# Merging the weight folds of a convolution chain into its pointwise stage, with the first bands of the large convolution loaded inside it

## The chip, the cores and the metric

One NeuronCore of a Trainium2 chip runs the whole program. The metric is device time in microseconds of one execution. Abbreviations: PE is TensorE, DVE is VectorE, ACT is ScalarE, POOL is GpSimd, SP is SyncE. SPq and ACTq in the rows are the sequencers of SyncE and ScalarE, which issue DMAs.

## The reference

Two layers over 16 images of 192 channels, 56 by 56, float32. Only the first layer's first step and its constants are touched here:

```python
y = jnp.einsum('bchw,oc->bohw', x, pw_w)
x_pw = bn(y, pw_g, pw_b, pw_m, pw_v) + x
out = bn(dwconv(x_pw, dwk_w), dwk_g, dwk_b, dwk_m, dwk_v)          # 13x13 depthwise
out = out + bn(x_pw * dw1_w.reshape(1, -1, 1, 1), dw1_g, dw1_b, dw1_m, dw1_v)
return jax.nn.gelu(out, approximate=False)
```

`bn` is y * g / sqrt(v + eps) + (b - m * g / sqrt(v + eps)). The second layer is an attention-like block: two norms, two small depthwise mixes (5x5, 3x3, 1x1 kernels summed), a recurrence and a feed-forward part. All of it stands behind the first layer.

## The kernel before

`build` calls the stages in order, each a block of its own with one instruction list for each engine; a block ends only when all engines are through, and the next begins then: `prepare`, `pointwise`, `depthwise` (the 13x13 convolution), norm scales, `omni`, `attention`, norm scales, `omni`, `feed_forward`.

`prepare` folds constants. SyncE issues 16 loads (L200), VectorE clears the flat tap tables (L214, L215), waits for all 16 loads on one semaphore, and folds: scales and shifts of the three norms (L224 to L229), the pointwise weights with scale and identity (L232, L234), the output weights (L236, L237), the 13x13 taps (L243), the 5x5 taps (L252 to L260), their edge sums (L267 to L273). Every step waits for the one before. ScalarE takes the roots and an exponential between (L281 to L284), waits for the last fold, and stores five tables and the bias row to DRAM (L286 to L291), as the later stages read them from there.

`pointwise` works image by image with two input buffers `xin` and two output buffers `xp` (2.41 MB an image each way). SyncE loads image b+2 when PE is through with image b. PE computes 14 pairs of columns an image, four products each (L334), into one of 7 PSUM banks (L301) in turn. VectorE adds the shift and moves the bank to `xp` (L347), which frees it; at the start of image b it first waits for the store of image b-2, which used the same `xp`. ScalarE waits for an image's last evacuation and issues its store to `xpw_d` (L359).

`depthwise` goes over 24 groups of 8 channels with two buffers. For each group SyncE loads the input (L418), the bias (L422) and the bands, which are overlapping windows of the flat tap table `f13_d` (two DMAs of 56 partitions, L133). It first waits until GpSimd has cleared the margins of the band buffers (L467). ScalarE rounds the bands (L516) and the input (L521) of the first channel after it has waited for all loads of the group, GpSimd makes the rests (L473, L477), and PE multiplies (L87 to L89).

The DMAs that SyncE issues go by one queue (q1 in the page), those of ScalarE by another (q10).

Of the kernel before, what the change touches and what calls it, by code (L numbers as in the profile page):

```python
# [141 lines left out]
def prepare(nc, ins, keep, wpw, shift_pw, f13_d, f5a_d, f5f_d, sa_d, sf_d, bias_d):  # L142

    with ExitStack() as ctx:
        m = Mem(nc, ctx)
        bcv = m.sb("bcv", [128, NV, C])
# [11 lines left out]
        run = m.sb("f5_running", [CT, 2, KT, 1 + l5])  # L158
        box = m.sb("f5_box", [CT, l5])
        edge = m.sb("f5_edge", [CT, 2, KT, n5])  # L160
        sd = m.sb("sd", [128, 3, C])
        sc = m.sb("sc", [128, 3, C])
        sh = m.sb("sh", [128, 3, C])
# [5 lines left out]
        loads = m.sem("prep_loaded")  # L169
        var_ready = m.sem("prep_variances")  # L170
        root = m.sem("prep_roots")
        step = m.sem("prep_steps")
        expo = m.sem("prep_exponentials")
        stored = m.sem("prep_stored")
        block = ctx.enter_context(nc.Block())
        folds = [0]

        @block.sync
        def _(sp):
            n = 0  # L180
            vecs = ins["vecs"]
            for dst, src in [
                (bcv[:, :, :], dram(vecs, 0, [[0, 128], [1, NV * C]])),
                (colv[:, :, :], ins["vec_cols"]),
                (alph[:, :], dram(ins["alphas"], 0, [[0, CT], [1, 8]])),
                (keep.ident[:, :], ins["ident"]),
                (wpw[:, :, :], ins["pw_wt"].rearrange("(k p) n -> p k n", p=CT)),
                (keep.w_low[:, :, :], ins["att_low"]),
                (keep.w_end[:, :, :], ins["att_ends"]),
                (keep.wo[:, :, 0:C], ins["att_out"]),  # L190
                (rates[:, :, :], ins["att_rates"]),
                (dwk[:, :, :], ins["dwk_w"].rearrange("(k p) n -> p k n", p=CT)),
                (w5[:, 0], ins["att_w5"].rearrange("(k p) n -> p k n", p=CT)),
                (w5[:, 1], ins["ffn_w5"].rearrange("(k p) n -> p k n", p=CT)),
                (w3[:, 0], ins["att_w3"].rearrange("(k p) n -> p k n", p=CT)),
                (w3[:, 1], ins["ffn_w3"].rearrange("(k p) n -> p k n", p=CT)),
                (w1[:, 0], ins["att_w1"]),
                (w1[:, 1], ins["ffn_w1"]),
            ]:
                sp.dma_start(dst, src).then_inc(loads, 16)  # L200
                n += 16
            folds[0] = n

        @block.vector
        def _(dve):
            done = [0]

            def link(ins_):

                done[0] += 1  # L210
                ins_.then_inc(step, 1)
                dve.wait_ge(step, done[0])

            link(dve.memset(f13[:, :, :], 0.0))  # L214
            link(dve.memset(f5[:, :, :, :], 0.0))  # L215
            dve.wait_ge(loads, folds[0])
            dve.tensor_scalar_add(sd[:, :, :], bcv[:, 0:3, :], BN_EPS).then_inc(var_ready, 1)
            dve.tensor_scalar_add(cd[:, :, :], colv[:, :, 0:3], BN_EPS).then_inc(var_ready, 1)

            link(dve.tensor_scalar_mul(keep.decay[:, :, :], rates[:, :, 0:2], 1.0 / HW))  # L220
            dve.scalar_tensor_tensor(uw[:, :, :], rates[:, :, 2:4], 1.0 / HW,
                                     keep.decay[:, :, :], ALU.mult, ALU.add).then_inc(var_ready, 1)
            dve.wait_ge(root, 2)
            link(dve.reciprocal(sd[:, :, :], sd[:, :, :]))  # L224
            link(dve.tensor_mul(sc[:, :, :], bcv[:, 3:6, :], sd[:, :, :]))
            link(dve.tensor_mul(sh[:, :, :], bcv[:, 9:12, :], sc[:, :, :]))
            link(dve.tensor_sub(sh[:, :, :], bcv[:, 6:9, :], sh[:, :, :]))
            link(dve.tensor_copy(shift_pw[:, :], sh[:, 0, :]))
            link(dve.tensor_add(sd[:, 0, :], sh[:, 1, :], sh[:, 2, :]))  # L229

            for k in range(KT):
                link(dve.tensor_mul(wpw[:, k, :], wpw[:, k, :], sc[0:CT, 0, :]))  # L232
                own = wpw[:, k, k * CT:(k + 1) * CT]
                link(dve.tensor_add(own, own, keep.ident[0:CT, 0:CT]))  # L234
            for n in range(3):
                link(dve.tensor_mul(keep.wo[:, n, 0:C], keep.wo[:, n, 0:C], bcv[:, V["gamma1"], :]))  # L236
            link(dve.tensor_reduce(keep.wo[:, :, C], keep.wo[:, :, 0:C], AX_X, ALU.add))  # L237

            link(dve.reciprocal(cd[:, :, :], cd[:, :, :]))
            link(dve.tensor_mul(cs[:, :, :], colv[:, :, 3:6], cd[:, :, :]))  # L240
            link(dve.tensor_mul(c1[:, :], colv[:, :, V["dw1_w"]], cs[:, :, 2]))
            for k in range(KT):
                link(dve.tensor_scalar(taps_view(f13[:, k, :], K13, c13),  # L243
                                       dwk[:, k, :].rearrange("p (a b) -> p a b", a=K13),
                                       cs[:, k, 1:2], None, ALU.mult))
                mid = f13[:, k, c13:c13 + 1]
                link(dve.tensor_add(mid, mid, c1[:, k:k + 1]))

            for s in range(2):
                a = [alph[:, 4 * s + n:4 * s + n + 1] for n in range(4)]  # L250
                for k in range(KT):
                    link(dve.tensor_scalar(taps_view(f5[:, s, k, :], K5, c5),  # L252
                                           w5[:, s, k, :].rearrange("p (a b) -> p a b", a=K5),
                                           a[3], None, ALU.mult))
                    inner = taps_view(f5[:, s, k, :], K3, c5)
                    link(dve.scalar_tensor_tensor(inner, w3[:, s, k, :].rearrange("p (a b) -> p a b", a=K3),
                                                  a[2], inner, ALU.mult, ALU.add))
                    mid = f5[:, s, k, c5:c5 + 1]
                    link(dve.scalar_tensor_tensor(mid, w1[:, s, k:k + 1], a[1], mid, ALU.mult, ALU.add))
                    link(dve.tensor_add(mid, mid, a[0]))  # L260

            link(dve.memset(run[:, :, :, 0:1], 0.0))
            for s in range(2):
                gain, bias = V[f"ln{s + 1}_g"], V[f"ln{s + 1}_b"]
                for k in range(KT):
                    taps = f5[:, s, k, :]
                    link(dve.tensor_tensor_scan(run[:, s, k, 1:1 + l5], taps, free(run[:, s, k, 0:1], [[0, l5]]), 0.0,  # L267
# [11 lines left out]
        def _(act):  # L279
# [12 lines left out]
            act.wait_ge(stored, 96)  # L292


def pointwise(nc, B, x, wpw, shift_pw, xpw_d):

    with ExitStack() as ctx:
        m = Mem(nc, ctx)
# [1459 lines left out]
```

## Time and profile before

| | us |
|---|---|
| median of 3 runs | 5809.89 |
| lowest, highest | 5807.37, 5811.38 |
| the profiled execution's own time | 5813.4 |
| span of the profiled execution, first to last instruction | 5811.6 |
| PE busy | 4955.2 (85%) |
| DVE busy | 3771.1 (65%) |
| POOL busy | 3556.7 (61%) |
| ACT busy | 3493.3 (60%) |

The profile is one execution. Busy time counts instructions in work, not waits. The share of an engine is an average over stages with different limits, so each stage is read by itself: the timeline shows instructions in order with the idle time before each and what ended it; the table of stretches gives the busy time of each engine, the granted clock of TensorE, the mean busy share of the 16 DMA engines and the bytes that they moved. A DMA's line shows when it was issued; the time from issue to landing stands apart.

### The profile page before, as it was taken

The page shows a single profiled execution, that of the slowest core. Times are in us where ns is not written, and L with a number is a line of the kernel's source. Part 1 is how long each engine was busy: PE and PEld are TensorE (multiplying, and loading weights), DVE is VectorE, ACT ScalarE, POOL GpSimd, SP SyncE. Part 2 cuts the span into 40 slices and gives each one's busy share as a digit, 9 for nine tenths or more (in the row PEclk, how much of TensorE's full clock was granted, in tenths as well). Part 3 has the DMA queues.
Part 4 walks back from the last instruction along what each step waited for, and adds up shares of the span by engine and source line. Part 5 has one row for each costly group of instructions (what it writes and reads, how often), then busy time and mean ns, then how long its engine had stood idle before and what let it go on. Part 6 is the DMA issues. An engine that isn't in the chain of part 4 may idle for free. (4 is left out here: it accounts for less than half of the span.)

```text
span 5811.6 us, 78329 instructions
## 1 busy us (share of the span) xinstructions
PE 4955.2 (85%) x23504; PEld 3915.4 (67%) x23504; DVE 3771.1 (65%) x5591; ACT 3493.3 (60%) x6892; POOL 3556.7 (61%) x2992
## 2 busy tenths in 40 slices
PE   5979999979966776766867764997999999999999
PEld 5969999967733343443433434776888888888888
DVE  4423333367769999999999994774555555555555
ACT  0017777746656776766767764665555556665555
POOL 0027777757768888888888882775444444444444
PEclk9989999989988888988989887998999999999999
DMA  6987777689830321312223115997223223222320
GB/s 167 264 209 198 184 197 183 163 208 260 249 84 20 82 56 45 84 45 73 67 55 80 45 34 142 263 263 183 56 56 89 56 58 84 60 56 72 73 55 25
DMA packets 388598, 674.50 MB, mean 116 GB/s; under 512 B 21117, under 2 KB 346702, under 8 KB 368910
## 3 DMA queue, kind: packets, MB, share of 16 engines
q1 hardware_dynamic: 334768, 514.71, 38.1%
q10 hardware_dynamic: 53522, 156.21, 7.2%
q8 instruction: 130, 2.13, 0.1%
q14 instruction: 178, 1.46, 0.1%
HBM read 437.00 MB, written 233.87 MB: 115 GB/s over the span
## 5 line engine op out<-in xcount | busy, mean ns | idle before, releaser
L1545 POOL TENSOR_TENSOR hidden_part<-hidden_whole,hidden_part 128x448 fp32r<-128x448 f32 x672 | 752.8, 1156 | 1030.7 <-ACT hidden_part L1510 1029.9
L676 POOL TENSOR_TENSOR omni_in_part<-omni_norm,omni_in_part 113x448 fp32r<-113x448 f32 x384 | 609.1, 1598 | 202.7 <-ACT omni_in_part L735 199.7
L1414 PE MATMUL f_out_ps<-hidden_part,ffn_wv_parts 128*128 128x448 f32 (+1 forms) x3360 | 721.5, 370 | 0.7 <-POOL hidden_part L1545 0.7
L1414 PEld LDWEIGHTS f_out_ps<-hidden_part,ffn_wv_parts 128*128 128x128 f32 (+1 forms) x3360 | 578.6, 177 | 103.9 <-POOL hidden_part L1545 33.5
L1588 DVE TENSOR_SCALAR hidden_whole<-f_hid_ps 128x448 f32<-128x448 f32 x672 | 417.6, 622 | 254.2 <-POOL hidden_part L1545 149.3
L1038 PE MATMUL proj_ps<-mixT_low,kvr_weights_low 128*128 128x448 f32 x672 | 360.9, 622 | 214.7 <-ACT k_all L1102 184.1
L87 PE MATMUL omni_ps<-omni_in_part,omni_band_part 113*112 113x448 f32 x1152 | 438.8, 381 | 113.0 <-POOL omni_in_part L676 78.9
L1040 PE MATMUL proj_ps<-mixT_ends,kvr_weights_ends 128*128 128x448 f32 x1008 | 519.7, 599 | 0.0
L87 PE MATMUL dw_ps<-dw_in_part,dw_band_part 112*112 112x432 f32 (+3 forms) x1344 | 474.4, 353 | 42.6 <-POOL dw_in_part L477 42.6
L1203 POOL TENSOR_TENSOR input_times_v<-input_factor,v_all 128x448 f32<-128x448 f32 x336 | 420.3, 1251 | 93.2 <-ACT input_factor L1107 74.3
L88 PE MATMUL dw_ps<-dw_in_part,dw_band_part 112*112 112x432 f32 (+3 forms) x1344 | 474.7, 353 | 0.0
L89 PE MATMUL dw_ps<-dw_in_part,dw_band_part 112*112 112x432 f32 (+3 forms) x1344 | 472.0, 351 | 0.0
L473 POOL TENSOR_TENSOR dw_band_part<-dw_band,dw_band_part 112x784 fp32r<-112x784 f32 x192 | 335.0, 1745 | 191.9 <-ACT dw_band_part L516 191.8
L88 PE MATMUL omni_ps<-omni_in_part,omni_band_part 113*112 113x448 f32 x1152 | 436.8, 379 | 0.0
L89 PE MATMUL omni_ps<-omni_in_part,omni_band_part 113*112 113x448 f32 x1152 | 436.4, 379 | 0.0
L494 DVE TENSOR_TENSOR dw_sums<-dw_sums,dw_out 112x448 f32<-112x448 f32 x192 | 121.5, 633 | 456.6 <-ACT dw_out L545 456.6
L1414 PE MATMUL f_hid_ps<-ffn_mixT_part,ffn_wk_high 128*128 128x448 f32 x1344 | 397.3, 377 | 7.6 <-DVE hidden_whole L1588 6.2
L1510 ACT ACTIVATE hidden_part<-hidden_whole 128x448 fp32r<-128x448 f32 x672 | 389.2, 579 | 21.3
L516 ACT ACTIVATE dw_band_part<-dw_band 112x784 fp32r<-112x784 f32 x192 | 163.6, 852 | 390.8 <-DMA dw_band<-flat 383.8
L1040 PEld LDWEIGHTS proj_ps<-mixT_ends,kvr_weights_ends 128*128 128x128 f32 x1008 | 194.9, 207 | 278.7 <-issue 278.7
L1508 ACT ACTIVATE hidden_whole<-hidden_whole 128x448 f32<-128x448 f32 x672 | 379.8, 565 | 3.6 <-DVE hidden_whole L1588 2.0
L1038 PEld LDWEIGHTS proj_ps<-mixT_low,kvr_weights_low 128*128 128x128 f32 x672 | 134.8, 213 | 359.8 <-ACT k_all L1102 218.6
(178 smaller groups left out, 13181.4 us busy)
## 6 DMA issues: line engine op xcount, KB each, us to landing
xin<-x SPq DMA_DIRECT2D x16, 2352.0 KB, 13.1
x_pointwise<-xp ACTq DMA_DIRECT2D x16, 2352.0 KB, 18.8
dw_in<-x_pointwise SPq DMA_DIRECT2D x24, 1568.0 KB, 24.4
y_gelu<-dw_out ACTq DMA_DIRECT2D x24, 1568.0 KB, 13.2
omni_in<-y_gelu SPq DMA_DIRECT2D x24, 1568.0 KB, 23.0
att_mix<-omni_out ACTq DMA_DIRECT2D x24, 1568.0 KB, 12.7
residual_pairs<-y_gelu SPq DMA_DIRECT2D x16, 2352.0 KB, 11.8
tok<-residual_pairs SPq DMA_DIRECT2D x16, 2352.0 KB, 9.0
```

The costliest lines, as they stand in the source:

```text
L87: pe.matmul(bank, w_hi, x_hi, start=start, stop=False)
L88: pe.matmul(bank, w_hi, x_lo, start=False, stop=False)
L89: return pe.matmul(bank, w_lo, x_hi, start=False, stop=stop)
L676: pool.tensor_tensor(rounded(inner(p[1])), z[u][:, :, cc, :], inner(p[0]), ALU.subtract).then_inc(in_split, 1)
L1038: pe.matmul(to[:, 0:TC], keep.w_low[:, o, 0:LOW], low[kind // 2], start=True, stop=False)
L1040: pe.matmul(to[:, 0:TC], keep.w_end[:, o, part * 128:(part + 1) * 128], x_end[:, t, :], start=False, stop=True).then_inc(bank_ready, 1)
L1203: pool.tensor_tensor(grid(EV[unit.slot % 2]), grid(E[unit.slot]), part_of(vS, unit), ALU.mult).then_inc(ev_done, 1)
L1414: return pe.matmul(bank, rounded(w), rounded(x), start=start, stop=stop)
L1508: act.activation(whole[h % KW][:, :], whole[h % KW][:, :], ACT.Square).then_inc(kk_ready, 1)
L1510: act.activation(rounded(kk[n % 2][0][:, h, :]), whole[h % KW][:, :], ACT.Copy).then_inc(kh_ready, 1)
L1545: pool.tensor_tensor(rounded(kk[n % 2][1][:, h, :]), whole[h % KW][:, :], kk[n % 2][0][:, h, :], ALU.subtract).then_inc(kl_ready, 1)
L1588: dve.tensor_scalar_max(whole[h % KW][:, :], hidden_bank(n, h)[:, 0:TC], 0.0).then_inc(relu_done, 1)
```

## The change

`prepare` and `pointwise` become one function and one block. The sync queue loads the norm rows, the pointwise weights and the identity, then at once images 0 and 1. VectorE folds only scale, weights and shift before the first image. The 14 other constants and one more table are loaded from the ScalarE queue. Their folds are put behind single evacuations of images 1 to 5 (`behind`): those six images are written out, the other ten stay in the loop. ScalarE takes the remaining roots and the exponential before it stores image 0; after the store of image 5 it stores the folded tables, waits until they have landed, and issues the bands of groups 0 and 1 of the large convolution, whose buffers are now allocated ahead of both stages (`FirstBands`) and whose margins GpSimd clears in the pointwise block. Only after that comes the store of image 6. The large convolution then starts with input and bias alone. The arithmetic stays the same, but for the row constants, which are computed on one partition where they are stored from one.

The folding steps that are moved as they are, and the old `prepare`, are left out here:

```diff
-def prepare(nc, ins, keep, wpw, shift_pw, f13_d, f5a_d, f5f_d, sa_d, sf_d, bias_d):
+def pointwise(nc, B, ins, keep, bands, xpw_d, f13_d, f5a_d, f5f_d, sa_d, sf_d, bias_d):
...
+        PEELED = 3
+        REST = 14
...
+            sp.dma_start(bn[:, :, :], dram(ins["vecs"], 0, [[0, 128], [3 * C, 4], [1, C]])).then_inc(norm_loaded, 16)
+            sp.dma_start(wpw[:, :, :], ins["pw_wt"].rearrange("(k p) n -> p k n", p=CT)).then_inc(weights_loaded, 16)
+            sp.dma_start(keep.ident[:, :], ins["ident"]).then_inc(weights_loaded, 16)
             load(sp, 0, 0)
             load(sp, 1, 1)
...
+            pe.wait_ge(weights_ready, 2 * KT)
             with pe.Fori(0, B // 2) as i:
...
+        @block.gpsimd
+        def _(pool):
+            bands.clear_margins(pool)
...
+            def pointwise_folds():
+                dve.wait_ge(norm_loaded, 16)
+                dve.tensor_scalar_add(scale[:, :], bn[:, 0, :], BN_EPS).then_inc(deviated, 1)
+                dve.wait_ge(deviated, 2)
+                link(dve.reciprocal(scale[:, :], scale[:, :]))
+                link(dve.tensor_mul(scale[:, :], bn[:, 1, :], scale[:, :]))
+                dve.wait_ge(weights_loaded, 32)
+                for k in range(KT):
+                    dve.tensor_mul(wpw[:, k, :], wpw[:, k, :], scale[0:CT, :]).then_inc(weights_ready, 1)
+                dve.wait_ge(weights_ready, KT)
+                for k in range(KT):
+                    own = wpw[:, k, k * CT:(k + 1) * CT]
+                    dve.tensor_add(own, own, keep.ident[0:CT, 0:CT]).then_inc(weights_ready, 1)
+                link(dve.tensor_mul(shift[:, :], bn[:, 3, :], scale[:, :]))
+                dve.tensor_sub(shift[:, :], bn[:, 2, :], shift[:, :]).then_inc(shift_ready, 1)
+                dve.wait_ge(shift_ready, 1)
+
+            def row_variances():
+                dve.wait_ge(rest_loaded, 16 * REST)
+                dve.tensor_scalar_add(rsd[:, :, :], rowv[:, 1:3, :], BN_EPS).then_inc(variances, 1)
...
+            def behind(b, jp):
+
+                if b == 1:
+                    if jp == 4:
+                        row_variances()
+                    elif jp == 6:
+                        row_shifts()
+                    elif jp == 8:
+                        column_scales()
+                    elif jp in (10, 11):
+                        large_taps(jp - 10)
+                elif b == 2 and jp % 3 == 0 and jp // 3 < 4:
+                    small_taps(*divmod(jp // 3, KT))
+                elif b in (3, 4) and jp < 12:
+                    s, (k, part) = b - 3, divmod(jp // 3, 2)
+                    if jp % 3 == 0:
+                        (edges, normed_taps)[part](s, k)
+                elif b == 5 and jp in (2, 5, 8):
+                    out_weights(jp // 3)
...
+            pointwise_folds()
+            link(dve.memset(f13[:, :, :], 0.0))
+            link(dve.memset(f5[:, :, :, :], 0.0))
+            link(dve.memset(run[:, 0:1], 0.0))
+            for b in range(2 * PEELED):
+                dve.wait_ge(stored[b % 2], (b // 2) * 16 + 16)
+                for jp in range(PAIRS):
+                    evacuate(b // 2, b % 2, jp)
+                    behind(b, jp)
+            with dve.Fori(PEELED, B // 2) as i:
                 for u in range(2):
                     dve.wait_ge(stored[u], i * 16 + 16)
                     for jp in range(PAIRS):
-                        dve.wait_ge(ps_ready, i * (2 * PAIRS) + (u * PAIRS + jp + 1))
-                        dve.tensor_tensor(
-                            xp[u][:, :, 2 * jp:2 * jp + 2],
-                            ps[jp % NB][0:PXC, 0:2 * C].rearrange("p (q c) -> p c q", q=2),
-                            free(shift_pw[0:PXC, :], [[1, C], [0, 2]]), ALU.add).then_inc(ps_free, 1)
+                        evacuate(i, u, jp)
...
+            act.wait_ge(deviated, 1)
+            act.activation(scale[:, :], scale[:, :], ACT.Sqrt).then_inc(deviated, 1)
...
+            for dst, src in [
+                (rowv[:, :, :], dram(vecs, 0, [[NV * C, 1], [1, 12 * C]])),
...
+                act.dma_start(dst, src).then_inc(rest_loaded, 16)
+            act.dma_start(keep.w_end[:, :, :], ins["att_ends"]).then_inc(folds_stored, 16)
+
+            act.wait_ge(variances, 2)
+            act.activation(rsd[:, :, :], rsd[:, :, :], ACT.Sqrt).then_inc(root, 1)
+            act.activation(cd[:, :, :], cd[:, :, :], ACT.Sqrt).then_inc(root, 1)
+            act.wait_ge(variances, 3)
+            act.activation(keep.bonus[:, :, :], uw[:, :, :], ACT.Exp).then_inc(expo, 1)
+
+            def store(i, u):
+                act.wait_ge(ps_free, i * (2 * PAIRS) + ((u + 1) * PAIRS + NB))
+                act.dma_start(pair_batch(xpw_d, B, i * 2 + u), by_group(xp[u])).then_inc(stored[u], 16)
+
+            for b in range(2 * PEELED):
+                store(b // 2, b % 2)
+            act.wait_ge(step, counted[0])
+            act.dma_start(f13_d.rearrange("(k p) n -> p k n", p=CT), f13[:, :, :]).then_inc(folds_stored, 16)
+            act.dma_start(f5a_d.rearrange("(k p) n -> p k n", p=CT), f5[:, 0]).then_inc(folds_stored, 16)
+            act.dma_start(f5f_d.rearrange("(k p) n -> p k n", p=CT), f5[:, 1]).then_inc(folds_stored, 16)
+            act.dma_start(sa_d.rearrange("(k p) n -> p k n", p=CT), edge[:, 0]).then_inc(folds_stored, 16)
+            act.dma_start(sf_d.rearrange("(k p) n -> p k n", p=CT), edge[:, 1]).then_inc(folds_stored, 16)
+            act.dma_start(bias_d, rsd[0:1, 0, :]).then_inc(folds_stored, 16)
+            act.wait_ge(folds_stored, 16 * 7)
+            act.wait_ge(bands.zeroed, 4)
+            for u in range(2):
+                bands.load_first(act, f13_d, u)
+            with act.Fori(PEELED, B // 2) as i:
+                store(i, 0)
+                store(i, 1)
...
+class FirstBands:
+
+    def __init__(self, m, name, k):
+        _, _, self.length, self.cols = band(k)
+        self.wt = [m.sb(f"{name}_band{u}", [PXC, G, self.cols]) for u in range(2)]
+        self.zeroed = m.sem(f"{name}_band_margins_zeroed")
+        self.loaded = [m.sem(f"{name}_band_loaded{u}") for u in range(2)]
+
+    def clear_margins(self, pool):
+        for u in range(2):
+            for margin in (slice(0, PITCH), slice(self.cols - W, self.cols)):
+                pool.memset(self.wt[u][:, :, margin], 0.0).then_inc(self.zeroed, 1)
+
+    def load_first(self, eng, f_d, u):
+        load_band_rows(eng, self.wt[u], f_d, u * (G * self.length), self.length, self.cols, self.loaded[u])
...
-            sp.wait_ge(zeroed, 4)
             for u in range(2):
                 load_input(place(u), u)
                 load_bias(place(u), u)
-                load_bands(place(u), u)
...
+                with ExitStack() as large:
+                    bands = FirstBands(Mem(nc, large), "dw13", K13)
+                    pointwise(nc, B, ins, keep, bands, xpw_d, f13_d, f5a_d, f5f_d, sa_d, sf_d, bias_d)
+                    depthwise(nc, B, "dw13", xpw_d, K13, f13_d, y_d, bias_d, (s1, s2), bands)
```

## Rows read from the trace of the kernel before

**Rows 1.** The page's 40 slices of the span: busy tenths of two resources.

```profile
PE   5979999979966776766867764997999999999999
...
DMA  6987777689830321312223115997223223222320
```

**Rows 2.** Timeline, all engines, first 72 us: start, length, engine, line, operation, [idle before].

```profile
0.74 0.40 SPq L200 DMA_DIRECT2D bcv<-vecs  x1
...
17.56 0.46 DVE L217 TENSOR_SCALAR sd<-bcv 128x576 f32<-128x576 f32 x1 [12.51 <-DMA w<-ffn_w]
...
18.95 3.75 DVE L224 RECIPROCAL sd<-sd 128x576 f32<-128x576 f32 x1 [0.58 <-ACT cd L282]
...
34.96 1.17 DVE L267 TENSOR_TENSOR_SCAN f_running<-f,f_running 96x484 f32<-96x484 f32 x1
...
48.37 0.17 DVE L275 TENSOR_SCALAR wkv_bonus<-wkv_bonus 128x4 f32<-128x4 f32 x1
...
54.14 0.99 ACTq L291 DMA_DIRECT2D dw_bias<-sd  x1
58.05 271.76 SPq L311 DMA_DIRECT2D xin<-x  x16
...
71.33 294.38 PE L334 MATMUL pw_ps<-pointwise_weights,xin 96*112 96x192 f32 x1792 [71.33 <-DMA xin<-x]
```

**Rows 3.** The same timeline later: evacuations by VectorE and the stores that ScalarE issues.

```profile
74.26 0.56 DVE L347 TENSOR_TENSOR xp<-pw_ps,pointwise_shift 112x384 f32<-112x384 f32 x1 [25.72 <-PE pw_ps L334]
...
92.75 0.56 DVE L347 TENSOR_TENSOR xp<-pw_ps,pointwise_shift 112x384 f32<-112x384 f32 x1 [0.74 <-PE pw_ps L334]
93.49 273.32 ACTq L359 DMA_DIRECT2D x_pointwise<-xp  x16
...
149.69 1.02 DVE L347 TENSOR_TENSOR xp<-pw_ps,pointwise_shift 112x384 f32<-112x384 f32 x2 [1.79 <-DMA x_pointwise<-xp]
```

**Rows 4.** Stretches: length, busy PE PEld DVE ACT POOL, granted clock, DMA share, GB/s.

```profile
49.00:57.00 8.00, 0.00 (x0) 0.00 (x0) 0.00 (x0) 0.00 (x0) 0.00 (x0) 1.00 0.86 257
59.00:79.00 20.00, 7.67 (x29) 7.44 (x30) 1.67 (x3) 0.00 (x0) 0.00 (x0) 1.00 1.02 236
80.00:93.00 13.00, 13.00 (x82) 13.00 (x81) 5.58 (x11) 0.00 (x0) 0.00 (x0) 1.00 0.00 0
130.00:141.00 11.00, 11.00 (x70) 11.00 (x69) 4.62 (x9) 0.00 (x0) 0.00 (x0) 1.00 0.99 228
141.00:147.00 6.00, 6.00 (x39) 6.00 (x38) 2.64 (x5) 0.00 (x0) 0.00 (x0) 1.00 1.07 342
...
387.00:403.00 16.00, 0.00 (x0) 0.00 (x0) 0.00 (x0) 0.00 (x0) 0.00 (x0) 0.50 0.98 197
412.00:423.00 11.00, 11.00 (x60) 10.07 (x59) 2.60 (x5) 8.07 (x12) 11.00 (x8) 1.00 0.90 181
```

**Rows 5.** Image loads (xin, first line) and stores (xp, second): issue to landing.

```profile
DMA to landing us min/median/max: 12.9/13.1/22.6
...
DMA to landing us min/median/max: 10.1/18.8/19.7
```

**Rows 6.** Timeline at the turn to the large convolution, columns as in Rows 2.

```profile
377.07 1.79 POOL L467 MEMSET dw_band<- 112x496 f32 x4 [376.62 <-POOLq L297]
...
378.89 0.34 SPq L418 DMA_DIRECT2D dw_in<-x_pointwise  x1
379.28 0.42 SPq L422 DMA_DIRECT2D dw_cols<-dw_bias  x1
...
404.25 0.86 ACT L516 ACTIVATE dw_band_part<-dw_band 112x784 fp32r<-112x784 f32 x1 [383.82 <-DMA dw_band<-flat]
...
408.32 0.68 PE L87 MATMUL dw_ps<-dw_in_part,dw_band_part 112*112 112x448 f32 x1 [42.61 <-POOL dw_in_part L477]
```

**Rows 7.** Landing of the first bias; then of the first two inputs (min, max).

```profile
DMA to landing us min/median/max: 9.8/9.8/9.8
...
DMA to landing us min/median/max: 8.1/17.8/27.5
```

More of the change, by code:

```diff
@@ L139, in by_group @@
     return t[:, :, :].rearrange("p (g c) j -> p g (c j)", g=NG)
-def prepare(nc, ins, keep, wpw, shift_pw, f13_d, f5a_d, f5f_d, sa_d, sf_d, bias_d):
+def pointwise(nc, B, ins, keep, bands, xpw_d, f13_d, f5a_d, f5f_d, sa_d, sf_d, bias_d):
     with ExitStack() as ctx:
         m = Mem(nc, ctx)
-        bcv = m.sb("bcv", [128, NV, C])
+        wpw = m.sb("pointwise_weights", [CT, KT, C])
+        shift = m.sb("pointwise_shift", [128, C])
+        scale = m.sb("pointwise_scale", [128, C])
+        bn = m.sb("pointwise_norm", [128, 4, C])
+        xin = [m.sb(f"xin{u}", [CT, KT, HW]) for u in range(2)]
+        xp = [m.sb(f"xp{u}", [PXC, C, PJ]) for u in range(2)]
+        NB = 7
+        ps = [m.ps(f"pw_ps{i}") for i in range(NB)]
+        rowv = m.sb("norm_rows", [1, 12, C])
+        gam = m.sb("gamma_rows", [128, C])
         colv = m.sb("colv", [CT, KT, NV])
@@ L168, in prepare @@
         rates = m.sb("rates", [128, 2, 4])
[L169 to L267, printed above, removed]
-                                                ALU.add, ALU.add))
-                    span = l5 + 1 - W
-                    link(dve.tensor_sub(box[:, 0:span], run[:, s, k, W:W + span], run[:, s, k, 0:span]))
-                    link(dve.tensor_add(edge[:, s, k, :], box[:, 0:n5], box[:, PITCH:PITCH + n5]))
-                    link(dve.tensor_scalar(edge[:, s, k, :], edge[:, s, k, :], colv[:, k, bias:bias + 1], None, ALU.mult))
-                    link(dve.tensor_scalar(taps, taps, colv[:, k, gain:gain + 1], None, ALU.mult))
-            dve.wait_ge(expo, 1)
-            link(dve.tensor_scalar_add(keep.bonus[:, :, :], keep.bonus[:, :, :], -1.0))
-            folds[0] = done[0]
@@ L295, in pointwise @@
-def pointwise(nc, B, x, wpw, shift_pw, xpw_d):
-    with ExitStack() as ctx:
-        m = Mem(nc, ctx)
-        xin = [m.sb(f"xin{u}", [CT, KT, HW]) for u in range(2)]
-        xp = [m.sb(f"xp{u}", [PXC, C, PJ]) for u in range(2)]
-        NB = 7
-        ps = [m.ps(f"pw_ps{i}") for i in range(NB)]
+        norm_loaded = m.sem("pw_norm_loaded")
+        weights_loaded = m.sem("pw_weights_loaded")
+        rest_loaded = m.sem("fold_inputs_loaded")
+        deviated = m.sem("pw_deviation")
+        variances = m.sem("rest_variances")
@@ L303, in pointwise @@
+        root = m.sem("rest_roots")
+        expo = m.sem("bonus_exponential")
+        step = m.sem("fold_steps")
+        shift_ready = m.sem("pw_shift_ready")
+        weights_ready = m.sem("pw_weights_folded")
+        folds_stored = m.sem("folds_stored")
         loaded = [m.sem(f"x_loaded{u}") for u in range(2)]
@@ L369, in depthwise @@
+def depthwise(nc, B, name, src, k, f_d, dst, bias_d, stats, bands):
     dmax, centre, length, cols = band(k)
@@ L374, in depthwise @@
         m = Mem(nc, ctx)
-        wt = [m.sb(f"{name}_band{u}", [PXC, G, cols]) for u in range(2)]
+        wt, w_loaded = bands.wt, bands.loaded
         raw = [m.sb(f"{name}_in{u}", [PXC, B, G, PJ]) for u in range(2)]
@@ L464, in _ @@
         def _(pool):
-            for u in range(2):
-                for margin in (slice(0, PITCH), slice(cols - W, cols)):
-                    pool.memset(wt[u][:, :, margin], 0.0).then_inc(zeroed, 1)
             with pool.Fori(0, NG // 2) as i:
```

115 lines of the change are left out of this document (79 added, 36 removed).

## The prediction, made before the changed kernel ran

> **What bounds the kernel now.** I read the page's slices first [rows 1]: PE is busy in nearly all of the 5811.6 us span, and what the change touches lies in its first three slices (435 us). DMA stands at 8 or 9 tenths there, at 1 to 3 in most later ones. The rest of the kernel should only shift, so I work out three things alone: when the pointwise stage starts, how long it runs, and how soon the large convolution follows.
>
> The timeline gives the start. VectorE waits for the last of 16 input loads until 17.56, folds until 48.54, the six fold stores are issued until 55.13 and must land, the block ends, the first image is only then requested at 58.05, and PE starts at 71.33 [rows 2]. Nothing of the main work runs before that.
>
> In the pointwise stage the bound is PE, narrowly. A pair of columns takes 1.30 us (evacuations repeat 0.56 busy, 0.74 idle, released by PE [rows 3]), so an image takes 14 x 1.30 = 18.2 us; image 0 takes 92.8 - 71.3 = 21.5, since its first pairs are slow (the first evacuation starts 2.9 us after PE). PE runs unbroken for 294.4 us, to 365.7 [rows 2]. DMA is the second bound just behind: while a load is in flight it moves 228 GB/s at share 0.99, then the store drains at 342 GB/s at 1.07 [rows 4]. A load (2.41 MB) alone runs at 236 GB/s, so it costs 10.2 to 10.6 us of all the engines; a store costs 2.41 MB / 342 = 7.0 us. Together 17.4 of each 18.2 us. That is why a store lands 18.8 us after its issue [rows 5] and VectorE sometimes waits for one at an image's start [rows 3]. Seven PSUM banks (L301) hide that: PE may run 7 x 1.30 = 9.1 us ahead of a blocked evacuation.
>
> At the turn PE ends at 365.7, the next block starts at 377.1, the loads go out at 378.9, ScalarE starts at 404.25, PE at 408.32 [rows 6].
>
> **Part 1, the front.** Removed from the path: 13 of the 16 loads ahead of the first fold, all folds but those of scale, shift and weights, the fold stores' landing, one block end. The sync queue now issues three small loads (0.6 MB) from 0.74 on and then image 0. At the 257 to 236 GB/s of [rows 4] the small ones need 2.4 us and image 0 10.2 us, after about 1 us to the first byte (issue at 58.05, a full stretch from 59 [rows 2, 4]) and with some 2.5 us between last byte and landing (58.05 + 13.1 against 59 + 10.2 [rows 5]): about 16. ScalarE issues 15 loads (1.46 MB) beside it, whose packets mix in; I add 1: **PE starts at 17.0**. Bounds: 15 (no mixing) and 22 (all 1.46 MB, at 257 GB/s 5.7 us, ahead of it). The folds for PE don't decide: the norm rows land near 5, the reciprocal shrinks from 576 to 192 elements (3.75 / 3 = 1.25 us [rows 2]), ten further short steps end near 11. Gain: 71.3 - 17.0 = **54.3 us**.
>
> **Part 2, folds between evacuations.** Their cover is the banks: VectorE has 0.74 us free per pair and 9.1 us of reserve. The longest insertion is the row shifts, one reciprocal of 384 elements (2.5 us, scaled) and four short ones, about 5 us; an edge step (a scan of 1.17 us [rows 2] and two shorter) takes 2.4 us in every third pair, alternating with 0.9, so 3.4 us per six pairs with 4.4 us free. Nothing reaches PE. If the 14 loads that it waits for land late, VectorE stands in image 1's fifth pair, at 44.5 by my clock; x0, x1 and all small loads together are 6.9 MB, 29 us at 236 GB/s, so they are there near 33. ScalarE is held too: store 0 now stands behind its wait for the variances, so it goes out near 48 instead of 39.3. Load 2 (from 38.5) holds the DMA until 49 anyway. Cost 0; without that cover 9 us at most.
>
> **Part 3, the early bands.** This takes the gain back. After store 5 ScalarE issues the fold stores (2.06 MB), waits for their landing, then issues the bands of both groups, and only then store 6. Bands cost much: 2.88 MB a group, 16 us at 197 GB/s and share 0.98, or 181 GB/s at 0.90 [rows 4]: 14.6 to 15.9, and from the first input's landing (378.9 + 8.1 [rows 6, 7]) to ScalarE's start at 404.2 it is 17.2. I take **32.7 us** for two (17.1 + 15.6), bounds 29 and 35. They are ahead of store 6 on one queue, which goes in order: the second dw input, issued behind the first bands at 381, took 27.5 us to land though its 1.6 MB need 4.5 [rows 7].
>
> By the clock of part 1 image 0 ends at 38.5, image 5 at 38.5 + 5 x 18.2 = 129.5, image 6 at 147.7, image 7 at 165.9. The DMA works without a gap from 130.5: load 7 10.4, store 5 7.0, folds 2.06 / 0.257 = 8.0 [rows 4], load 8 10.4: 166.3. The folds finish among the last of these and have landed near 167. From 167: load 9 10.4, bands 32.7, store 6 7.0: 217.1, landed 1.5 later, 218.6. Image 8 can't be evacuated before that (same buffer as image 6), and PE has run out of banks at 165.9 + 9.1 = 175.0. Stall: 218.6 + 0.6 for the first evacuation - 175.0 = **44.2 us**. PE then restarts as at 71.33, 21.5 - 18.2 = 3.3 us slower; **+47.5 us**. Bounds with the restart: 34 (folds landed 9 us earlier because their packets pass load 8's, bands at 29) to 53 (bands 35, a store at the 10.1 - 1.5 = 8.6 of the one that ran alone [rows 5], 1.6 for gaps between issues). Later images need 17.4 of 18.2 us again. Image 15 ends at 219.2 + 9.1 + 3.3 + 7 x 18.2 = 359.0, only 6.7 us earlier than now.
>
> A rule of the Trainium skill speaks against this part (DMA: Bandwidth & Descriptors, section "Issuing engines are not separate DMA queues"): DMAs started by the scalar and the sync engine run on the same 16 DMA engines and interleave, and a second issuer saves only issue time. The trace agrees: the pending store makes no headway while a load moves at 228 GB/s. By the rule the bands cost their 32.7 us in this stage; were the queues separate, they would cost nothing there.
>
> **Part 4, the turn.** The stage's end to the next block's start stays 11.4 us (365.7 to 377.1). Then: no wait for the margins (377.07 + 1.8 = 378.9 [rows 6]), input and bias alone ahead of the first group. The bias, issued 0.4 us behind the input, lands 9.8 us later, so 10.2 us in all [rows 6, 7]; ScalarE to PE takes 408.32 - 404.25 = 4.1. PE starts 14.3 us after the block instead of 31.25: **17.0 us** gained. Bounds 12 (input slower beside the second) and 18. Both margin memsets and their semaphore lie under the pointwise front: 0.
>
> **Sum.** -54.3 + 47.5 - 17.0 = **-23.8 us**. The profiled run took 5813.4 us (span 5811.6), 3.5 above the median 5809.9; forecast 5809.9 - 23.8 = **5786 us** (a profiled run near 5790). Own range: front -56 to -49, stall and restart +34 to +53, turn -18 to -12: 5770 to 5802.
>
> **The rivals.**
> - *Bands and image loads overlap.* If the x loads' 228 GB/s is their own limit and not the engines', bands beside load 9 fill up to the 342 of the store's drain: 8.17 MB / 342 = 24 us instead of 43.1. Sum -43: 5767. Against it: share 0.99 with a store waiting [rows 4]. Chance 0.14.
> - *The bands are free*, hidden in the 0.8 us spare per image and the idle time before the last store: -71.3, 5739. 32.7 us don't fit into 7 x 0.8 with store 6 behind them. 0.05.
> - *The early bands don't bring the convolution forward*: the change then doesn't do what it says, as when the second input, now right behind the first, shares the engines with the bias and a split step waits for it. Turn gains 0: -6.8, 5803. For it: the second bias took long in the queue; against it: 8.1 and 9.8 us for the first [rows 7]. 0.12.
> - *Slower than before*: the bands cost a multiple while x packets alternate with theirs and the store behind them waits for all of it. The gains are 71.3 us, so stall and restart must exceed 71, bands of 57 us, to lose at all, and 83 to lose measurably. At three times the price (98 us) the sum is +41.5: 5851. Against it: the first bands ran at nearly the same price with the queue full. 0.06.
>
> **How the numbers follow.** Forecast 0.63, rivals 0.14, 0.05, 0.12, 0.06. A measurement here tells 0.2% (11.6 us) from nothing. Faster: 0.60 of the forecast's 0.63 (its upper end passes 5798), 0.14 and 0.05: 0.79. Same: 0.03 + 0.12 = 0.15. Slower: 0.06. The range takes the forecast's likely part and the first and third rival: 5754 to 5805; left out are free bands, the slower case and tails, some 0.17.
>
> **What would show it.** Right: PE's first matmul near 17; loads and the first three or four stores as now; one wait of VectorE for a store at image 8, some 43 us, with PE idle from near 175 to 219, DMA share 0.9 to 1.0 and GB/s near 180 to 230 in it; image 15 near 359; from the turn's block start to PE 14.3 us instead of 31.25. Wrong: a first matmul after 22; PE idle in images 1 to 5 (folds not covered); no stall, or one above 60; a turn still near 31.

## The result: 0.27% slower, and the profile after

The changed kernel takes 5824.62 us (median of 8 runs, 5818.55 to 5828.81), the kernel before 5808.63 us (8 runs, 5801.77 to 5816.21). The ratio is 1.0027, with a 95% interval of 1.0017 to 1.0037. The forecast was 24 us faster; it came out 16 us slower.

Yet the part that the prediction worked out went nearly as it said. These are the front, the wait at image 8 and the turn in the timeline of the changed kernel (start, length, engine, line, operation, [idle before]):

```profile
2.19 60.33 SPq L200 DMA_DIRECT2D xin<-x  x4
...
21.90 158.39 PE L227 MATMUL pw_ps<-pointwise_weights,xin 96*112 96x192 f32 x952 [21.90 <-DMA xin<-x]
...
135.78 13.20 ACTq L403 DMA_DIRECT2D flat<-f  x1
...
170.54 10.64 ACTq L133 DMA_DIRECT2D dw_band<-flat  x4
181.52 180.87 ACTq L398 DMA_DIRECT2D x_pointwise<-xp  x10
...
221.67 3.35 DVE L343 TENSOR_TENSOR xp<-pw_ps,pointwise_shift 112x384 f32<-112x384 f32 x7 [49.88 <-DMA x_pointwise<-xp]
...
222.28 139.01 PE L227 MATMUL pw_ps<-pointwise_weights,xin 96*112 96x192 f32 x840 [41.99 <-DVE xp L343]
...
372.66 0.33 SPq L488 DMA_DIRECT2D dw_in<-x_pointwise  x1
...
382.91 0.86 ACT L581 ACTIVATE dw_band_part<-dw_band 112x784 fp32r<-112x784 f32 x1 [329.51 <-DMA dw_cols<-dw_bias]
...
386.98 0.69 PE L87 MATMUL dw_ps<-dw_in_part,dw_band_part 112*112 112x448 f32 x1 [25.69 <-POOL dw_in_part L542]
```

Read it against [rows 2, 3, 6]. PE (in the line at 21.90) starts at 21.9 instead of 71.3. It runs without a gap until 180.3 (21.90 + 158.39), so the folds between evacuations cost it nothing. Then it stands still for 42.0 us: the bands go out at 170.5, store 6 only at 181.5, behind them, and the first evacuation of image 8 waits for it. The convolution's first product comes at 387.0 instead of 408.3, so at this point the changed kernel is 21.3 us ahead.

While PE waits, the DMA engines are full. The table of stretches of the changed kernel (columns as in [rows 4]):

```profile
182.00:196.00 14.00, 0.00 (x0) 0.00 (x0) 0.00 (x0) 0.00 (x0) 0.00 (x0) 0.52 0.92 198
196.00:212.00 16.00, 0.00 (x0) 0.00 (x0) 0.00 (x0) 0.00 (x0) 0.00 (x0) 0.50 0.94 194
212.00:221.00 9.00, 0.00 (x0) 0.00 (x0) 0.00 (x0) 0.00 (x0) 0.00 (x0) 0.50 1.00 292
```

The lead holds until the last stage: the first product of feed-forward's hidden layer is at 4004.2, and at 4024.9 before. Then it is lost, and more. The stage as one stretch, first of the kernel before, then of the changed one:

```profile
4025.00:5811.00 1786.00, 1773.43 (x9400) 1539.86 (x9400) 963.71 (x1566) 1062.08 (x2021) 752.77 (x672) 1.00 0.26 64
```

```profile
4004.00:5823.00 1819.00, 1784.75 (x9400) 1551.25 (x9400) 963.75 (x1567) 1062.94 (x2021) 753.04 (x672) 0.99 0.26 63
```

The same 9400 matmuls take 33 us more in a stage whose code the change doesn't touch. The table of waits in this stage says where (engine, tile, line, what it waited for: us in all, times, longest). Before:

```profile
DVE f_out_ps L1583 <- issue: 12.3, 5, 2.5
...
PE f_hid_ps L1414 <- DVE hidden_whole L1588: 6.2, 6, 1.2
```

The changed kernel:

```profile
PE f_hid_ps L1479 <- DVE hidden_whole L1653: 28.5, 12, 4.2
...
DVE hidden_whole L1653 <- issue: 26.8, 6, 4.8
DVE f_out_ps L1648 <- issue: 12.3, 5, 2.6
```

"issue" is a wait for nothing that the profile shows. Both kernels have the waits of 2.5 us at L1583 and L1648, where VectorE's first work behind the loop's head stands. Only the changed one has six more, of 4.5 us on average, a few instructions later, one each time the loop jumps back to its head (seven passes, six jumps). One of them in its timeline, with the loads that SyncE issues at the same time:

```profile
4229.99 0.42 SPq L1687 DMA_DIRECT2D ffn_mix<-ffn_mix  x1
4230.50 4.43 SPq L1688 DMA_DIRECT2D ffn_tok<-tok  x1
```

```profile
4231.12 0.62 DVE L1648 TENSOR_TENSOR f_out_ps<-f_out_ps,ffn_r_rest 64x448 f32<-64x448 f32 x1 [2.58 <-issue]
4231.67 0.60 DVE L1653 TENSOR_SCALAR hidden_whole<-f_hid_ps 128x448 f32<-128x448 f32 x1
4236.46 1.16 DVE L1653 TENSOR_SCALAR hidden_whole<-f_hid_ps 128x448 f32<-128x448 f32 x2 [4.18 <-issue]
```

Around it PE is half idle and its clock falls to the lower of its two levels, 0.50 of full. The stretch around the wait, and one form of matmul ahead of the wait and behind it:

```profile
4230.00:4240.00 10.00, 5.13 (x18) 3.98 (x17) 2.83 (x5) 3.88 (x7) 2.75 (x3) 0.71 1.04 234
```

```profile
4232.84 0.36 PE L1479 MATMUL f_hid_ps<-ffn_mixT_part,ffn_wk_rest 128*128 128x448 f32 x1
...
4238.05 0.57 PE L1479 MATMUL f_hid_ps<-ffn_mixT_part,ffn_wk_rest 128*128 128x448 f32 x1
```

The two together make up the 33 us: PE waits 22.3 us longer for L1653 (28.5 against 6.2), and its busy time for the same 9400 matmuls is 11.3 us longer (1784.75 against 1773.43).

The page of the changed kernel also counts the DMAs that bring instructions (packets, MB, share):

```profile
q14 instruction: 179, 1.47, 0.1%
```

1.47 MB in 179 packets is 8.2 KB each.

### The profile page after: what moved, and what is told of

Read it like the earlier page. It is cut to its first block and busy times, and to the rows that moved or that the text cites. A ratio compares the mean times of both kernels' runs of the same rounds, so it can differ in the third digit from the quotient of the medians.

```text
span 5823.6 us, 78234 instructions
## 1 busy us (share of the span) xinstructions
PE 4973.1 (85%) x23504; PEld 3931.4 (68%) x23504; DVE 3765.9 (65%) x5597; ACT 3494.0 (60%) x6893; POOL 3551.2 (61%) x2992
## 3 DMA queue, kind: packets, MB, share of 16 engines
q8 instruction: 130, 2.13, 0.2%
q14 instruction: 179, 1.47, 0.1%
## 5 line engine op out<-in xcount | busy, mean ns | idle before, releaser
L1653 DVE TENSOR_SCALAR hidden_whole<-f_hid_ps 128x448 f32<-128x448 f32 x672 | 417.6, 622 | 287.3 <-POOL hidden_part L1610 149.2
L1479 PE MATMUL f_hid_ps<-ffn_mixT_part,ffn_wk_high 128*128 128x448 f32 x1344 | 403.4, 382 | 28.5 <-DVE hidden_whole L1653 28.5
L1575 ACT ACTIVATE hidden_part<-hidden_whole 128x448 fp32r<-128x448 f32 x672 | 389.0, 579 | 21.3
```

Source lines behind the costliest of these rows:

```text
L1479: return pe.matmul(bank, rounded(w), rounded(x), start=start, stop=stop)
L1575: act.activation(rounded(kk[n % 2][0][:, h, :]), whole[h % KW][:, :], ACT.Copy).then_inc(kh_ready, 1)
L1653: dve.tensor_scalar_max(whole[h % KW][:, :], hidden_bank(n, h)[:, 0:TC], 0.0).then_inc(relu_done, 1)
```

## The theory and its rival

**Theory, fetch position.** VectorE's instructions are brought in pieces by DMA. I assume that a piece is one packet of 8.2 KB and holds 128 instructions (64 bytes each). The change lengthened VectorE's list: in the built programs 4830 of its instructions stand ahead of the feed-forward loop's head before, and 4941 after, 111 more, by the six images written out and the folds between them. So everything behind stands 111 instructions, or 17 short of a whole piece, elsewhere. At a turn of the loop VectorE fetches the piece with the loop's head (the 2.5 us that both have). Where the piece ends a few instructions later, the next one is needed at once, and its fetch stands behind 4.7 MB of image loads. Where it ends later, the fetch is done in time.

The packet records of the same trace bear on this. VectorE stops at 4228.5; one packet of q14 is read from 4229.0 to 4229.6, and VectorE goes on at 4231.1. It stops again at 4232.3; the next packet of q14 is read only from 4234.1 to 4234.7, while the image loads fill the DMA engines, and VectorE goes on at 4236.5. The queues in the stretch 4234.0 to 4234.8 (packets, MB, share):

```profile
q1 hardware_dynamic: 173, 0.16, 109.9%
q14 instruction: 1, 0.01, 5.0%
```

It is so in all fourteen traces of this case. VectorE has 78 waits for "issue" of over 0.5 us in feed-forward; each has exactly one q14 packet of 8192 bytes in it or just ahead of it, and VectorE goes on 1.3 to 1.8 us after the packet was read.

**Rival.** Something else in the change slows the later stages: the lower clock (0.934 over the span instead of 0.940), other addresses of tiles and tables, the longer list as such. ScalarE's list changed too.

## Experiments on the lost 33 us

### The position put back, without touching anything else

```diff
             def pointwise_folds():
+                for _ in range(17):
+                    dve.sem_inc(pad, 1)
                 dve.wait_ge(norm_loaded, 16)
```

> The changed kernel with 17 empty semaphore increments put ahead of VectorE's first fold, in time that VectorE spends waiting. Its instruction list is 111 longer than before's ahead of the feed-forward loop; 17 more make it 128 longer, 8 KB, the size of one of VectorE's instruction fetches in the trace. Theory (fetch position): in the changed kernel VectorE reaches the end of a fetched piece a few instructions after the feed-forward loop's head, and the next fetch queues behind the image loads issued just then; it stood idle 6 times for 26.8 us there, which before's trace does not have. With the pad the position is that of before: feed-forward back to before's length, so the 33 us come back and the time is 5787 (before - 21, the gain at the first convolution's start). Rival (the clock or the memory addresses make the later stages slower): no change from the changed kernel, 5824.

Measured: 5781.27 us, ratio to before 0.9955 (0.9941 to 0.9968). Seventeen instructions that do nothing make the changed kernel 43 us faster, 6 more than the 37 expected. In the profiled executions feed-forward is 39 us shorter, and the stages ahead of it are 9 us shorter, for which the theory has no reason. ScalarE's list is as in the changed kernel, so it was not the cause. In the waits of this kernel's VectorE only the old kind is left:

```profile
DVE f_out_ps L1651 <- issue: 12.5, 5, 2.7
```

### The changed kernel's position given to the kernel before

```diff
+            for _ in range(111):
+                dve.sem_inc(pad, 1)
             link(dve.memset(f13[:, :, :], 0.0))
```

> The kernel before with 111 empty semaphore increments on VectorE ahead of its first fold, where it waits for loads until 17.6 us anyway. Theory (fetch position): every later VectorE instruction stands where it stands in the changed kernel, so feed-forward gets the same waits at each turn of its loop: 33 us slower, 5842; at most 5 us of it at the start. Rival (the later stages suffer from something else in the change): 5809 to 5812.

Measured: 5840.20 us, 1.0052 (1.0038 to 1.0065). The old kernel, with nothing of the change but its position, loses 31 us. The changed kernel's addresses and its other edits are not in it, and its clock is 0.938 as in e1, so they are not the cause. The waits are in the same place:

```profile
DVE hidden_whole L1591 <- issue: 26.7, 6, 4.8
```

### Two other positions

> The changed kernel with 8 empty VectorE increments instead of 17. In the changed kernel's trace VectorE stood still after the 5th instruction of the feed-forward loop; if a fetched piece of 128 instructions ends there, 8 more put the head of the loop 3 instructions behind a piece's start, with 125 to go before the next fetch is needed. Theory (fetch position): no such wait, 5781 as with 17. Rival (only the exact position of before is free of it, or the 17 helped by something else): between 5781 and 5824, above 5795.

Measured: 5783.61 us, 0.9958 (0.9942 to 0.9975; four runs, 5770.75 to 5789.42), and no wait for issue at the hidden layer. Eight are as good as seventeen within this spread, so it is not before's exact place that helps, nor the sum of 128.

> The kernel before with 64 empty VectorE increments instead of 111. By the count of instructions the feed-forward loop's head then has 52 instructions left in its fetched piece, at 2 a us in this loop some 25 us, while the loads last 22. Theory (fetch position): no waits, 5810. Rival (any longer list ahead costs time, as the 111 did): 5825 or more.

Measured: 5808.18 us, 1.0001 (0.9991 to 1.001). A longer list as such costs nothing. The waits at the hidden layer come to 1.7 us in all:

```profile
DVE f_out_ps L1586 <- issue: 9.8, 4, 2.7
...
DVE hidden_whole L1591 <- issue: 1.7, 7, 0.3
```

### The loads moved away from the fetch

The changed kernel at its bad position; only the image loads of feed-forward's turn go out a chunk later.

```diff
                     if t == NCH - 1 and reload:
+                        if u == 1:
+                            sp.wait_ge(res_done, i * (CH * 2) + (2 * n + 2 + 2 + 2))
                         load(i * 2 + (u + 2), u)
```

> The changed kernel without any pad, with one wait added far behind it: at the turn of the feed-forward loop SyncE issues the next two image loads (4.7 MB) one chunk later, some 17 us, so that they don't go out while VectorE fetches the head of its loop. Theory (the second fetch is slow only because it stands behind these loads): the six waits of 4.5 us shrink to under 1, feed-forward returns to before's length, 5791, or some us over it for what the moved loads meet. Rival (the fetch at that position takes 4 us by itself, or what is slow has nothing to do with the loads): 5824.

Measured: 5789.64 us, 0.996 (0.9945 to 0.9974), where 5791 was expected. The pieces end where they did and VectorE still runs out, but the waits are short:

```profile
DVE hidden_whole L1653 <- issue: 6.1, 5, 1.3
```

The packets show what was delayed. At a turn of this run VectorE goes on behind the loop's head at 4452.5, and the next packet of q14 is read from 4453.0, 0.5 us later. In the changed kernel it goes on at 4231.1, and the next packet is read from 4234.1, 2.9 us later.

So both are needed: a position at which VectorE runs out right behind the loop's head, and loads issued at that moment. Two things stay open. The loads moved away at a good position were not tried, so what that move does by itself isn't known. And the six positions (none, 8 and 17 added to the changed kernel, none, 64 and 111 to the one before) fit a piece of 256 instructions as well as one of 128, and none of them puts the bad position one piece further on. For the shorter piece speaks that a single packet of 8.2 KB ends each wait.

## Experiments on the pointwise stage

All of these have the 17 increments, so they compare with 5781 us; their edits are shown without them.

### Both groups' bands at the turn again

```diff
-            for u in range(2):
-                bands.load_first(act, f13_d, u)
...
                 load_input(place(u), u)
                 load_bias(place(u), u)
+                load_bands(place(u), u)
```

> The padded changed kernel with the bands of both groups loaded at the start of the large convolution again, by SyncE, behind input and bias. Theory (the early bands cost more than they bring): the 42 us in which PE waits at image 8 and the slow restart of 3 us go, the turn gets its 17 us back: 28 us less than the padded changed kernel, 5760 (before - 49); the convolution's first product near 359. Rival (bands cost nothing in the stage and the wait at image 8 is for the folds' landing): stall stays near 40, turn 17 longer, so 5805.

Measured: 5767.16 us, 0.9929 (0.9914 to 0.9945), 14 us less than with early bands, where 28 was expected (5760). The bands loaded early do cost more than they bring, but by half of that: PE still waits 11.5 us at image 8, where store 6 goes out at 167.3, only after the fold stores have landed. Its waits:

```profile
PE dw_ps L87 <- POOL dw_in_part L543: 40.2, 1, 40.2
...
PE pw_ps L228 <- DVE xp L346: 11.5, 1, 11.5
```

### Both groups' bands behind the last image load

```diff
                     load(sp, i * 2 + (u + 2), u)
+            sp.wait_ge(folds_stored, 16 * 7)
+            sp.wait_ge(bands.zeroed, 4)
+            for u in range(2):
+                bands.load_first(sp, f13_d, u)
```

The early loads by ScalarE are taken out.

> The padded changed kernel with both groups' bands issued by SyncE behind the last image load, inside the pointwise block, instead of by ScalarE ahead of store 6. Theory (the stage is full of DMA work, and only the order decides who waits): no wait at image 8; the bands' 32.7 us share the engines with stores 13 to 15, of 64 us of DMA work left when load 15 is issued 47 would fit under PE, so the block ends some 17 us later than without bands and the turn saves 17: 5760, as e3. Rival (only the place ahead of store 6 was bad, the stage has room): the convolution starts 17 earlier than in e3, 5743.

Measured: 5775.17 us, 0.9944 (0.9928 to 0.9959), worse than e3 by 8 us, where the same 5760 was expected, and far from the rival's 5743. PE waited in two places, 29.7 us in all: 10.4 at image 8, as in e3, and 19.3 ahead of the last 56 matmuls, behind the bands. So the place ahead of store 6 was not alone at fault: neither of the two places has room for 5.8 MB.

### Group 0's bands alone early

```diff
-            for u in range(2):
-                bands.load_first(act, f13_d, u)
+            bands.load_first(act, f13_d, 0)
...
                 load_bias(place(u), u)
+                if u == 1:
+                    load_bands(place(u), u)
```

> The changed kernel padded by 17 (5781), with the bands of group 0 alone loaded early by ScalarE, those of group 1 at the turn behind its input. Theory (each group's bands cost 16.4 us of DMA work ahead of store 6, and only group 0's are on the path at the turn): PE waits 23.6 us at image 8 instead of 40.0, the turn stays at 25.6: 5765. Rival (the wait is set by latencies, not by the bytes ahead of store 6): wait near 40, 5781.

Measured: 5766.92 us, 0.9927 (0.9911 to 0.9944). 5765 was expected. PE's wait falls from 40.0 (e1) to 25.3 us (23.6 expected), and the turn keeps its short form:

```profile
PE dw_ps L87 <- POOL dw_in_part L546: 25.7, 1, 25.7
PE pw_ps L228 <- DVE xp L346: 25.3, 1, 25.3
```

The wait goes by the bytes ahead of store 6: 14.7 us for a group's 2.88 MB.

### The wait for the folds' landing taken from ahead of store 6

```diff
-            act.wait_ge(folds_stored, 16 * 7)
...
                 store(i, 1)
+            act.wait_ge(folds_stored, 16 * 7)
```

The bands of both groups are at the turn, as in e3.

> Bands at the turn as in e3_bands_at_turn (5767, where PE still waited 11.5 us at image 8), but ScalarE waits for the fold stores' landing only at the end of the block, not ahead of store 6. Theory (store 6 was ready at 148 and went out only when the folds had landed behind load 8): the wait of 11.5 us goes, 5756. Rival (the folds' 8 us of DMA work delay store 6 anyway, as the queue goes in order): half of it or more stays, 5762.

Measured: 5767.21 us, 0.9928 (0.9912 to 0.9945), no different from e3 and above both expectations (5756 and the rival's 5762). PE's wait was 7.6 us instead of 11.5, so more than half of it stayed, as the rival said. Store 6 is issued at 153.4 instead of 167.3, but it takes 31.0 us to land: ScalarE's queue (q10) still moves fold stores, and then load 8 comes between. With the folds spread (e11 below) there is no wait at image 8.

### The constants behind image 0

```diff
+            act.wait_ge(loaded[0], 16)
             vecs = ins["vecs"]
```

> The changed kernel padded by 17, whose first matmul was at 20.5 us in its profile, with one edit: ScalarE issues the 14 constants (and one more table) only after image 0 has landed. Theory (their many small packets share the engines with image 0, 5 us of the front): first matmul at 17, 3.5 us less in all, 5778; the constants land before image 1's fifth pair at 45, so nothing else moves. Rival (image 0 is late for another reason, the small loads cost nothing): first matmul still at 20.5, 5781.

Measured: 5780.59 us, 0.9949 (0.9933 to 0.9966), with the first matmul at 19.2. Kernels with the same front and the constants in their old place had it at 19.1 to 21.9, so the time alone settles little. The queues up to the first matmul say more. In the changed kernel (until 21.9):

```profile
q1 hardware_dynamic: 1169, 4.32, 91.1%
q10 hardware_dynamic: 167, 0.11, 2.9%
```

The constants (q10) had moved 0.11 MB by then. The small loads and image 0 are 3.0 MB of q1's 4.32, so 1.3 MB of image 1, issued right behind image 0, were read ahead of image 0's landing.

### Two versions from the findings

Both load group 0's bands alone, by SyncE behind the last image load, and group 1's at the turn. Both also have the edits of e5 and e6: the constants behind image 0, the wait for the folds' landing at the end of the block.

> A version from the findings, padded by 17: bands of group 0 alone issued by SyncE behind the last image load, those of group 1 at the turn, the wait for the folds' landing at the block's end, the constants after image 0. Theory (DMA work decides): the folds cost a wait of 7.6 us and a restart as in e6, group 0's 16.4 us fit beside the last three images, and the turn is the short one: the convolution starts near 350, 5749. Rival (SyncE's bands hold up the last stores as in e4): near 360, 5759.

Measured: 5756.23 us, 0.9905 (0.9889 to 0.9922). PE waited twice, 14.7 us in all: 8.2 at image 8 for the folds and 6.4 ahead of the last 56 matmuls. The convolution started at 358.4. Time and start lie nearer to the rival's 5759 and 360 than to 5749 and 350.

The second version spreads the fold stores as well:

```diff
+            for b in range(B):
+                store(b // 2, b % 2)
+                if b == 5:
+                    act.wait_ge(step, counted[0])
+                if 5 <= b < 5 + len(folded):
+                    act.dma_start(*folded[b - 5]).then_inc(folds_stored, 16)
+            act.wait_ge(folds_stored, 16 * 7)
```

> As e7_group0_after_loads, but the six fold stores are spread, one behind each of the stores of images 5 to 10, at most 0.75 MB at a time. Theory (8 us of folds in one piece exceed what the 7 banks and the 0.8 us spare per image cover, 2 us at a time do not): no wait of PE in the stage, the convolution starts near 340, 5740. Rival (the spare time is used up, so that the lag adds up over the images): a wait of PE of 5 us or more later in the stage, 5749.

Measured: 5746.64 us, 0.9894 (0.9878 to 0.9911), the best here: 62 us less than before and 78 less than the change as it was made. The convolution starts at 348.4, where the theory said 340 (5740) and the rival's time was 5749. The wait at image 8 is gone. One is left, ahead of the last 56 matmuls, where e7 has 6.4 us with the folds in one piece; so it comes with group 0's bands and not, as the rival had it, from folds that add up:

```profile
PE dw_ps L87 <- POOL dw_in_part L550: 26.0, 1, 26.0
...
PE pw_ps L231 <- DVE xp L349: 6.0, 1, 6.0
```

## Why the prediction was wrong

**The step that failed** is in its first paragraph: "The rest of the kernel should only shift". Nothing in the sum had a term for it. The rest shifted by 21 us up to 4004 and then took 33 us more, for a reason that no rival named: the 111 instructions that the change adds to VectorE's list put a fetch right behind feed-forward's loop head, beside 4.7 MB of loads. The prediction looked at the six images written out only for what they do in their own stage. With the position put back the measured time is 5781 us, 5 off the forecast of 5786 and inside its range.

**The sum** at the convolution's start was -21.3 us instead of -23.8. That is near, but in part by luck, as two errors go against each other: the front gained 49.4 (54.3 forecast), stall and restart cost 45.0 (47.5), the turn gained 16.9 (17.0).

**The front** was forecast at 17.0 with an upper bound of 22; it was 21.9 in the profiled run and 18.7 to 21.5 in the others. Image 0 took 19.6 us from its issue at 2.2 to landing, where the sum allowed 14.8. The sum had 1 us for ScalarE's constants, of which only 0.11 MB moved in that time; it had nothing for image 1, of which 1.3 MB moved instead. In the kernel before, 3.00 MB in all moved while image 0 was loaded, 0.6 of them image 1's, and those are contained in the 13.1 us that the sum started from. The other 0.7 MB are some 3 of the missing 5 us, an estimate at the 213 to 238 GB/s of that stretch; the rest is open.

**The folds between evacuations** cost nothing, as said: PE is unbroken through images 1 to 5, VectorE's longest absence (53.4 to 58.1, the row shifts) stays inside the banks' 9.1 us.

**The wait at image 8** was put at 44.2 us and was 42.0, by the route that was given: folds behind load 8, bands behind the folds, store 6 behind the bands, share 0.92 to 1.00 all along. The price of the bands is near (14.7 us a group by e10, 16 in the sum). What it didn't say, though it follows from the same sum, is that the folds' stores exceed the spare time by themselves: 7.6 us of wait are left in e6 without any bands.

**The turn** came out as forecast: 11.4 us from PE's end to the first load of the next block (361.3 to 372.7), 14.3 us from there to the first product (372.7 to 387.0).

**The rivals.** That bands and loads overlap, or that the bands are free, fell with the 42 us. That the turn gains nothing fell with the 14.3. The time came out on the side of the slower rival, but not by its mechanism: the bands did not cost a multiple.

**The rule of the Trainium skill** cited there (DMA: Bandwidth & Descriptors, "Issuing engines are not separate DMA queues") is borne out by e4 as well: bands issued from the other queue, at another time, displaced stores all the same: 19.3 us of wait behind them, where the early ones cost 28.5 (40.0 in e1 less the 11.5 of e3). What the prediction should have drawn on stands on another page of the Trainium skill, Runtime: NRT & Kernel Launch, section "Instruction fetch mechanics": each engine fetches its instructions in blocks by a DMA queue of its own, and a taken branch to a block that is not held forces a fetch before execution goes on. The trace agrees on the jump: one packet of q14 is read in each wait of 2.5 us at the loop's head. Whether each engine has a queue of its own it doesn't show, as it tells only two apart, q8 and q14. The page gives blocks of 16 KiB, 256 instructions; the packets of q8 have that size (130 packets, 2.13 MB), those of q14, which end VectorE's waits, are 8.2 KB. It doesn't say that a fetch can be held up by the kernel's own loads; the runs with the loads moved and not moved show that, waits of 1.2 us against 4.5.

## What to carry to other kernels

A change that adds instructions to one engine moves every later loop of that engine, and a loop whose head lies a few instructions before the end of a fetched piece paid here at each turn, as large loads went out at that moment: look for "issue" waits right behind loop heads, in all stages, before a verdict on a change, and try a few empty instructions as a control. A pointwise stage that keeps the DMA engines at share 1.0 has no room for "early" transfers: in its middle a group's bands cost 14.7 us, nearly all of their 16, behind the last load 6.4. Only what lies on the path at the next stage's start (here one group's bands) is worth moving. In such a stage small pieces, spread over the images, cost less than one block (the folds: 8.2 us of wait in one piece in e7, none in e11).

## What was not expected of the hardware

Seventeen instructions without work changed the time by 43 us, 0.75%. At the loop's head VectorE waited 2.4 to 2.7 us for its first piece in every version. For the second one it waited 4.5 us where 4.7 MB of loads had just been issued, and 1.2 us without them (6.1 us in 5 waits). VectorE goes on only 1.3 to 1.8 us after the packet was read, with loads or without; what the loads delay is when the packet is read. Each of the six waits cost the stage 5.5 us (33 / 6), more than its own length: by the two sums above, a third of it is slower matmuls, as PE's granted clock fell to 0.50 in the wait.
